# A graph layer kernel whose setup stage loads its inputs in the order of need, counts edges first, and writes and reads back its edge ranges in the first pass

## The reference

```
xn = layernorm(x)
h = xn @ W.T;  e = leaky_relu((h @ a_src)[src] + (h @ a_dst)[dst])
gnn = xn + elu(segment_sum(softmax_per_dst(e)[:, None] * h[src], dst) + bias)
mix = linear_attention(xn, Wqkv, temperature) @ Wproj.T + bproj
x = x + gnn + mix
x = x + ffn(layernorm(x))        # top 2 of 8 experts, each 512 -> 256 -> 512
```

## Time and profile before

| what | value |
|---|---|
| median of 3 runs | 2663.34 us (2662.54 to 2670.57) |
| the profiled execution, own time | 2659.24 us |
| its span | 2657.5 us |
| PE busy | 2448.4 us (92%) |
| mean granted TensorE clock | 0.973 |
| setup stage, up to the first instruction of the first pass | 47.4 us |
| first pass, up to the first instruction of the next stage | 243.0 us (47.4 to 290.4) |

### The profile page before, as it was taken

How to read it: one execution, slowest core, us unless ns; L and a number is a source line. 1 busy time by engine, 2 the same in 40 slices (tenths; PEclk the granted TensorE clock), 3 DMA queues, 4 the chain that set the end, 5 groups by cost and what they waited for, 6 DMA issues and landing times. The chain is left out here.

```text
span 2657.5 us, 53246 instructions
## 1 busy us (share of the span) xinstructions
PE 2448.4 (92%) x12032; PEld 1387.5 (52%) x12033; DVE 1613.6 (61%) x4099; ACT 910.5 (34%) x1595; POOL 1238.8 (47%) x1258
## 2 busy tenths in 40 slices
PE   3999899999999888999999999999999849999995
PEld 2555566776666422333444444444444437777773
DVE  2555455564322144556666666666666676889986
ACT  0333344442111100001212222333333446777774
POOL 1444530000000277777777665555555214767774
PEclk9999899999999899999999999999999959999998
DMA  4333733331001377777777676666666475777775
GB/s 179 124 129 125 100 113 99 99 99 44 24 24 36 100 205 214 214 213 226 237 244 238 215 219 203 208 203 209 198 191 190 145 265 103 131 127 133 130 131 81
DMA packets 170291, 409.84 MB, mean 154 GB/s; under 512 B 38973, under 2 KB 39005, under 8 KB 169154
## 3 DMA queue, kind: packets, MB, share of 16 engines
q0 software_dynamic: 90512, 280.63, 39.8%
q1 hardware_dynamic: 51298, 76.55, 10.2%
q10 hardware_dynamic: 28368, 51.41, 5.6%
HBM read 339.66 MB, written 68.82 MB: 154 GB/s over the span
## 5 line engine op out<-in xcount | busy, mean ns | idle before, releaser
L1058 POOL DMA_INDIRECT rows<-h_rows,src_col x784 | 782.3, 998 | 477.9 <-PE acc_ps L1166 229.7
L1166 PE MATMUL acc_ps<-rows,W 128*128 x1776 | 836.5, 610 | 56.2 <-DVE W L1264 29.8
L1166 PEld LDWEIGHTS acc_ps<-rows,W 128*128 128x128 f32 x1776 | 310.4, 190 | 522.3 <-issue 521.5
L1264 DVE TENSOR_SCALAR W<-window,dst_col,w_col 128x128 f32<-128x128 f32 x888 | 298.8, 370 | 313.2 <-PE acc_ps L1166 261.2
L1611 POOL DMA_INDIRECT out<-y,token_of x105 | 168.5, 1605 | 115.1 <-issue 46.4
L1097 ACT ACTIVATE a_sd<-a_mv,cst 128x1 f32<-128x1 f32 x49 | 14.4, 295 | 591.8 <-DVE a_mv L1330 591.8
L651 POOL DMA_DIRECT2D alpha_d<-score x1 | 0.6, 573 | 461.6 <-DVE score L969 461.6
L1653 PE MATMUL o_ps<-w,hidT 128*128 x420 | 202.8, 605 | 8.5 <-DVE z L1713 2.7
L1643 PE MATMUL hid_ps<-xsT,w_now 128*128 128x128 f32 x1680 | 206.6, 277 | 0.2 <-issue 0.2
L1643 PEld LDWEIGHTS hid_ps<-xsT,w_now 128*128 128x128 f32 x1680 | 197.6, 193 | 1.0 <-issue 1.0
L775 PEld LDWEIGHTS q_ps<-hxnT,wqkv 128*128 128x128 f32 x1568 | 182.5, 193 | 12.0 <-issue 12.0
(11 more groups left out here) (301 smaller groups left out, 3430.7 us busy)
## 6 DMA issues: line engine op xcount, KB each, us to landing
lo_row<-src_lo SPq DMA_DIRECT2D x98, 256.0 KB, 3.3
xb<-in_x SPq DMA_DIRECT2D x49, 256.0 KB, 2.7
h_rows<-kb SPq DMA_DIRECT2D x49, 256.0 KB
fold_w<-in_x SPq DMA_DIRECT2D x49, 256.0 KB
rows<-h_rows,src_col POOLq DMA_INDIRECT x784, 3.7
a_own<-h_rows ACTq DMA_DIRECT2D x49, 256.0 KB, 3.8
a_xr<-in_x ACTq DMA_DIRECT2D x49, 256.0 KB, 5.2
out<-a_x ACTq DMA_DIRECT2D x49, 256.0 KB, 4.6
```

The costliest lines, as they stand in the source:

```text
L1058: nc.gpsimd.indirect_dma_start(G[:, n % ROWS, :], None, h_rows, bass.IndirectOffsetOnAxis(ap=src_col[:, n:n + 1], axis=0)).then_inc(row_in ...
L1166: nc.tensor.matmul(acc_ps[s][:], W[:, j, :], G[:, ds(row, 1), :].rearrange("p o d -> p (o d)"), start=(opens and j == 0), stop=(j == VT - ...
L1264: nc.vector.tensor_scalar(W[:, j, :], window[:], dst_col[:, ds(at_tile + j, 1)], w_col[:, ds(at_tile + j, 1)], ALU.is_equal, ALU.mult).the ...
```

## The change

The 13 loads come in another order and count up four semaphores: `first_in` (`last_i`, `cst`), `loaded` (five: `lin_i`, `src_row`, `dst_i`, `dst_row`, `last_bc`), `u_in` (`avec`, `w_nat`), `wg_in` (`wg`), and behind the write of zeros `wqkv_in` (`temp`, `src_col`, `wqkv`). DVE begins when `first_in` is complete and waits for `loaded` before it cuts the indices. PE does the tally and its prefix sums first and `u` behind them. The write of the ranges and the read back move from the end of the setup stage into SP's stream of the first pass, behind its load of tile 3 and of tile 5, and the buffer `rout_i` is kept for it. The first pass's end waits for the read back and for `wqkv_in`; PE waits for `wg_in` before its first product with `wg`.

```
-                        for dst, src in ((cst[:], a["consts"]), (wg[:], a["wg"]), (w_nat[:], a["w_nat"]),
-                                         (wqkv[:], a["wqkv"]), (avec[:], a["avec"]),
-                                         (temp[:], a["temp"]), (src_col[:], a["src_col"]),
-                                         (dst_i[:], a["dst_col"]), (lin_i[:], a["src_lin"]), (src_row[:], a["src_row"]),
-                                         (dst_row[:], a["dst_row"]), (last_i, a["last_col"]), (last_bc[:], a["dst_last"].partition_broadcast(NT))):
+                        for dst, src in ((last_i, a["last_col"]), (cst[:], a["consts"])):
+                            sp.dma_start(dst, src).then_inc(first_in, 16)
+                        for dst, src in ((lin_i[:], a["src_lin"]), (src_row[:], a["src_row"]), (dst_i[:], a["dst_col"]),
+                                         (dst_row[:], a["dst_row"]), (last_bc[:], a["dst_last"].partition_broadcast(NT))):
                             sp.dma_start(dst, src).then_inc(loaded, 16)
+                        sp.dma_start(avec[:], a["avec"]).then_inc(u_in, 16)
+                        sp.dma_start(w_nat[:], a["w_nat"]).then_inc(u_in, 16)
+                        sp.dma_start(wg[:], a["wg"]).then_inc(wg_in, 16)
                         sp.wait_ge(nothing_ready, 1)
                         sp.dma_start(starts_d[0:EP, :].rearrange("(p e) k -> p (e k)", p=P), nothing).then_inc(zero_out, 16)
+                        for dst, src in ((temp[:], a["temp"]), (src_col[:], a["src_col"]), (wqkv[:], a["wqkv"])):
+                            sp.dma_start(dst, src).then_inc(wqkv_in, 16)
                         sp.wait_ge(ints, 2)
                         sp.dma_start(src_lo.rearrange("(p c) -> p c", p=LC), lin_lo[:]).then_inc(saved, 16)
-                        sp.wait_ge(ints, 18)
-                        sp.dma_start(ranges_d, rout_i[:, 0:2]).then_inc(saved, 16)
-                        sp.wait_ge(saved, 32)
-                        sp.dma_start(ranges[:], ranges_d.rearrange("(o t) c -> o (t c)", o=1)).then_inc(r_loaded, 16)
-                        sp.wait_ge(r_loaded, 16)
+                        sp.wait_ge(saved, 16)
                         sp.wait_ge(zero_out, 16)
...
                     def _(pe):
-                        pe.wait_ge(loaded, 208)
...
                     def _(dve):
-                        dve.wait_ge(loaded, 208)
+                        dve.wait_ge(first_in, 32)
...
                         assert count.n == 4
+                        dve.wait_ge(loaded, 80)
...
                                 sp.dma_start(xb[s][:], a["x"][ds(t * P, P), :]).then_inc(x_in[s], 16)
+                                if isinstance(t, int) and t == XR + 1:
+                                    sp.wait_ge(r_saved, 16)
+                                    sp.dma_start(ranges[:], ranges_d.rearrange("(o t) c -> o (t c)", o=1)).then_inc(r_loaded, 16)
                                 if isinstance(t, int) and t == XR - 1:
+                                    sp.dma_start(ranges_d, rout_i[:, 0:2]).then_inc(r_saved, 16)
                                     sp.dma_start(gbias, a["gbias"].partition_broadcast(P)).then_inc(g_in, 16)
...
+                        sp.wait_ge(r_loaded, 16)
+                        sp.wait_ge(wqkv_in, 48)
...
                                 pe.wait_ge(hb_ready, t + 1)
+                                if isinstance(t, int) and t == 0:
+                                    pe.wait_ge(wg_in, 16)
```

More of the change, by code:

```diff
@@ L236, in gps_layer @@
             wproj_in = sem("wproj_in")
+            rout_i = sb(sc, "rout_i", [NT, 4], I32)
+            first_in, u_in, wg_in, wqkv_in, r_saved, r_loaded = (sem(n) for n in ("first_in", "u_in", "wg_in", "wqkv_in", "range_saved", "range_loaded"))
             pj = ExitStack()
@@ L256, in gps_layer @@
             rout = sb(ps, "rout", [NT, 8])
-            rout_i = sb(ps, "rout_i", [NT, 4], I32)
             loaded = sem("setup_loaded")
@@ L260, in gps_layer @@
             saved = sem("setup_saved")
-            r_loaded = sem("range_loaded")
             tri = sem("range_offsets")
@@ L312, in _ @@
                         nc.tensor.matmul(all_ps[:, 0:NT], C["ones_row"], tally, start=True, stop=True).then_inc(tally_done, 1)
+                        pe.wait_ge(u_in, 32)
+                        for k in range(KC):
+                            for j in range(KC):
+                                last = nc.tensor.matmul(u_ps[:, 2 * k:2 * k + 2], w_nat[:, j, k * P:(k + 1) * P],
+                                                        avec[:, j, :], start=(j == 0), stop=(j == KC - 1))
+                        last.then_inc(u_done, 1)
                         pe.wait_ge(ints, 14)
```

## The result

The changed kernel takes 2644.36 us, the median of 4 runs (2642.44 to 2648.06); beside it the kernel before took 2665.62 (4 runs, 2662.54 to 2670.57). The two medians are 21.3 us apart. The ratio is 0.9924, with a 95% interval of 0.991 to 0.9938: a gain of 20.3 us, between 16.5 and 24.0. The prediction was 2644.5 us and a gain of 18.8.

The account below looks back on a forecast made before the run. The setup stage's DMA queue was taken to bound: 26.9 + 0.4 + 0.6 = 27.9 us, plus 0.7 for the barrier, 28.6 instead of 47.37. So 2663.34 - 18.8 = 2644.5 us, range 2641 to 2648 (73%), whole range 2637 to 2651.

Parts of the forecast that it names:

- the queue: Setup stage's DMA loads: same bytes in another order, `src_lo` landing last at 27.9 us, bounds 27.4 to 29.2.
- both terms added to 26.9: Setup queue: 0.4 us for issuing `last_i` ahead of `cst`, and 0.6 us for `src_lo` behind the full queue.
- The chain: DVE and PE steps of the setup stage: end at 24.1 to 26.6 us, before the queue's 27.9.
- The ranges: Write and read back moved into SP's first pass: 4.5 us leave the setup stage, with no wait for the write.
- Rival 1: Setup stage: queue runs faster and the chain sets the end, gain 20 to 22.6 us, 2641 to 2643; 12%.
- The estimate from the Trainium skill's figure: Setup loads: 2.0 us plus bytes over 436 GB/s gives 23.6 us for 9.43 MB, below the chain's end.
- Rival 2: Setup stage: SP stopped in issuing, `wqkv` late and queue dry, gain 14 to 17 us, 2646 to 2649; 10%.
- Rival 3: First pass: a setup transfer, above all `wqkv`, still runs and delays loads of x, 5 to 8 us given back; 3%.
- Rival 4: First pass: PE meets the lower granted clock, 1.2 GHz; 60 us there cost 30, giving 2674 us; 2%.
- PE's slow first products: First pass: first eight products took 5.24 us, next eight 3.70; the slow time may shift 1.5 us either way.
- The sum: First pass's first load moves from 47.37 to 28.6 us, gain 18.8, bounds 17.5 to 19.3; later stages unchanged.

Follow-up runs that it names:

- e5: Changed kernel with the load of `wqkv` issued behind the write of `src_lo` instead of ahead of it; ratio 0.9914 to the kernel before.
- e1: Kernel before with only the ranges' write and read back moved into the first pass, loads in the old order; ratio 0.9988, 3.2 us.
- e2: Changed kernel with the ranges' write and read back put back at the end of the setup stage; ratio 0.994 to the kernel before.
- e8: Kernel of e5 with DVE's tally copy moved ahead of its wait for `loaded` and the index steps; ratio 0.9916 to the kernel before.
- e6: Changed kernel with the load of `wqkv` issued in the first pass, behind the bias load; ratio 0.9933 to the kernel before.
- e9: Kernel of e5 run again without an edit; ratio 0.9913 to the kernel before.
- e7: Changed kernel run again without an edit; ratio 0.9924 to the kernel before.

## Why the prediction was right

- **What sets the end of the stage: the queue.** `src_lo` landed at 27.8 us (27.9 predicted), 0.6 us behind `wqkv`'s 27.3, so both terms added to 26.9, 0.4 and 0.6, held. e5 shows the cause: with `wqkv` behind it the wait shrinks from 8.9 to 1.5 us. For this order the total stayed as assumed; the loads' rates moved with the loads.
- **The chain.** `first_in` at 6.4 us (6.2), `loaded` at 12.0 (10.6 to 13.1), `u` from 15.5 (14.4 to 16.9), the end at 24.7 (24.1 to 26.6). `off_ps` stood 2.4 us behind what it needed (2.7), covered by the queue.
- **The ranges.** No wait for `range_saved`, and the pass is 243.3 and 241.9 us long (243.0, 242.9 before). How this part's worth was put, as 4.5 us of landings leaving the stage, was too simple. On its own it is 3.0 to 3.7 us (e1), since DVE works on for 2 us beside the write; under the new order it is 3.4 us for another reason, the write's place behind the queue (e2).
- **Rival 1, a faster queue:** no; 9.39 MB until 27 us. The estimate from the Trainium skill's figure (DMA: Bandwidth & Descriptors, "Anatomy of one DMA") was 23.6 us for the train. The page fits that figure to one transfer issued by POOL, and here are 15 on SP's queue; the trace shows 27.8, so for this train of mixed short and long rows it was too low by 4.
- **Rival 2, SP stopped in issuing:** it did not happen at all. No issue took over 0.65 us, with as many transfers ahead as before.
- **Rival 3, a transfer running on into the first pass:** not in the changed kernel. In e5 and e8, where the loads of x are queued behind `wqkv`, the first statistics come 3.3 and 5.3 us behind the first load of x, against 2.7 in the changed kernel, so the mechanism that I named is real. In e6 the larger loss, 4.1 us, came with a late gather of POOL, which I had not named. The longer pass in e9 (245.8 us) shows nothing of it by itself, since e5 is the same kernel and its pass took 242.4.
- **Rival 4, the clock:** 1.00 in the first pass's stretch from 100 to 150 us, as before, and also over the whole pass.
- **PE's slow first products:** the first eight with `wg` took 4.70 us, and 4.98 in e7, against 5.24 and 4.65 in the two profiles before. So the 1.5 us allowed for them either way was more than they moved.
- **The sum.** 18.8 us were forecast for the stage, and the traces show 18.9 (17.6 between the second profiles: 46.69 and 29.05). The timed 20.3 us, 16.5 to 24.0, holds this; the 1.5 us between are within the interval, and nothing in the traces shows where they would be. That the median fell within 0.2 us of the forecast is luck: the gain came out 1.5 us or more larger than forecast, and the kernel before took 2665.62 us beside it and not the 2663.34 that the forecast started from. The profiled execution shows how wide the spread is: forecast at 2640.4 us, it took 2648.06, the longest of the four, while the 2659.24 that this forecast started from was shorter than every run timed beside it.

## What to carry to other kernels

Where a stage ends in a barrier, draw up its queue and its compute chain as two trains and predict the longer: a reordering of loads by need gains up to the moment the queue itself is the longer, and from there only what is queued ahead of the last needed transfer counts. A small write that the barrier waits for belongs ahead of the largest load, and a small write with a read back belongs in a stage where its queue is short. Moving a large load into the next stage need not be free even when nobody waits for it (e6 gave back the 3 us it had won): ask whose small gathers share the DMA engines.

## What the hardware showed that I had not expected

- A 392-byte write issued behind a long queue landed 7.0 us after its issue (e2). No packet was moved after 27.5 us, and it landed at 29.7, 2.2 us later. With an empty queue, before, its packets had gone by 42.6 us and it landed at 44.1, 1.5 us later. So in both, the last 1.5 to 2.2 us of the wait were not for the moving of its bytes. `src_lo`, 196 KB, landed at 27.8 in the changed kernel, with its last packets moved by 27.4.
- The 12th and 13th loads took 4.5 and 3.6 us to issue where the long rows of `wqkv` were issued fourth (before and e1), and 0.5 us where they were issued last, with as many transfers in front. The cause wasn't tried.
- Two profiles of the same kernel differ by 5.9 us in the edge loop, 1283.7 and 1289.6, at nearly the same granted clock (0.97 and 0.96 over the loop). A difference of spans from single profiles said 11 us where the stage's own rows said 19.
